# Two message-passing layers over 100,000 nodes: the destination rows gathered in the first pass, and its segment sums in another bank

## The reference, cut to what matters

```
h = relu(layernorm(x))                       # every node
f_s, f_v = linear maps of h                  # lin1
msg  = products of f[src], edge_attr, MLP(edge scalars)
mid  = segment_sum(msg, dst) / 4
conv = linear map of mid                     # lin2
angle = 0.1 * (mid_s @ lin3) / sqrt(96) * attr
x = x + cos(angle) * (linear map of h) * attr + sin(angle) * conv
h = relu(layernorm(x))
m = products of h[src], edge_attr, five weight matrices
x = x + h + relu(linear map of segment_sum(m, dst))
```

## Time and profile before

| | |
|---|---|
| time, median of 3 runs | 2462.75 us (2461.12 to 2464.57) |
| profiled execution | 2464.93 us, span 2463.1 us |
| busy: PE, DVE, ACT, POOL | 1773.9, 1866.4, 1350.1, 1483.3 us |
| mean granted clock of TensorE | 0.89 |

### The profile page before, as it was taken

The page is one execution under the profiler, slowest core; times in us unless marked ns, Lnnn a source line. Parts: engine busy times, 40 slices in busy tenths (PEclk is TensorE's granted clock), DMA queues, the critical chain, the costliest instruction groups (busy, mean ns, idle before and its releaser), DMA issues. The chain is left out here.

```text
span 2463.1 us, 51415 instructions
## 1 busy us (share of the span) xinstructions
PE 1773.9 (72%) x12130; PEld 1620.2 (66%) x12130; DVE 1866.4 (76%) x6716; ACT 1350.1 (55%) x3801; POOL 1483.3 (60%) x1436
## 2 busy tenths in 40 slices
PE   6788888888888888888886544545444777777776
PEld 2777777777777777777775544444444666666665
DVE  1799999999999999999996766666664555656554
ACT  2466666666666666666665645555553444444443
POOL 2345455454555545555454777777776777767775
PEclk9999999999999999999998555555555999999999
DMA  5355555555555555555554333333333333333332
GB/s 184 128 188 206 200 192 193 185 205 200 195 194 184 203 200 198 194 182 202 200 201 165 118 107 113 113 116 121 116 107 93 99 97 105 108 102 109 108 105 72
DMA packets 162656, 376.27 MB, mean 153 GB/s; under 512 B 42142, under 2 KB 72092, under 8 KB 162462
## 3 DMA queue, kind: packets, MB, share of 16 engines
q1 hardware_dynamic: 115582, 301.58, 34.7%
q0 software_dynamic: 47040, 74.31, 11.4%
HBM read 182.72 MB, written 200.80 MB: 156 GB/s over the span
## 5 line engine op out<-in xcount | busy, mean ns | idle before, releaser
L651 POOL TENSOR_TENSOR yo<-x,h 128x640 f32<-128x640 f32 x196 | 303.7, 1550 | 506.0 <-ACT h L774 504.8
L985 PE MATMUL bank<-wp,hT 128*128 128x160 f32 x1568 | 376.3, 322 | 0.0
L774 ACT ACTIVATE h<-x,nmr,inv 128x160 f32<-128x160 f32 x784 | 342.1, 514 | 1.5 <-DVE nmr L1211 1.5
L985 PE MATMUL bank<-wp,eT 128*128 128x160 f32 x784 | 263.6, 429 | 49.9 <-ACT eR L897 43.7
L610 POOL DMA_INDIRECT out<-yo,i_put x196 | 209.1, 1067 | 119.2 <-issue 80.7
L604 POOL DMA_INDIRECT x_e<-in_xa,i_src x196 | 217.3, 1109 | 98.7 <-issue 47.2
L1354 DVE SCALAR_TENSOR_TENSOR x<-bank,scl,x_all 128x160 f32<-128x160 f32 x784 | 256.3, 365 | 5.1 <-PE bank L986 2.6
L610 POOL DMA_INDIRECT h_all<-h,i_put x196 | 223.9, 1142 | 59.8 <-issue 58.6
L986 PE MATMUL bank<-wp,hR 128*128 128x64 f32 x1568 | 259.3, 247 | 0.0
L986 PEld LDWEIGHTS bank<-wp,hR 128*128 128x128 f32 x1568 | 255.5, 190 | 0.0
L980 PE MATMUL bank<-ident,h_e 128*128 128x128 f32 x392 | 83.6, 351 | 223.4 <-DVE hr_e L1526 223.0
(11 more groups left out here) (163 smaller groups left out, 5537.8 us busy)
## 6 DMA issues: line engine op xcount, KB each, us to landing
x_all<-in_xa SPq DMA_DIRECT2D x98, 644.0 KB, 5.0
h_all<-h SPq DMA_DIRECT2D x98, 640.0 KB, 3.0
out<-yo SPq DMA_DIRECT2D x98, 640.0 KB, 3.4
q_row<-row_tab SPq DMA_DIRECT2D x98, 256.0 KB, 3.6
sum_tab<-tot SPq DMA_DIRECT2D x49, 322.0 KB, 4.2
y_tab<-yo SPq DMA_DIRECT2D x49, 320.0 KB
x<-y_tab SPq DMA_DIRECT2D x49, 320.0 KB
cv<-sum_tab SPq DMA_DIRECT2D x25, 322.0 KB, 3.1
```

What stands on the lines that cost most here:

```text
L651: nc.gpsimd.tensor_tensor(yo[j][:, a:b], x1[j][:, a:b], h1[j][:, a:b], ALU.add).then_inc(d_y, 1)
L774: ins = nc.scalar.activation(h1[j][:, k * D:(k + 1) * D], x1[j][:, k * D:(k + 1) * D], ACT.Relu, bias=nmr2[j][:, k:k + 1], scale=inv2[j][: ...
L985: nc.tensor.matmul(dst_ps, main[:, t * P:(t + 1) * P], wp[:, w:w + D], start=True, stop=False)
```

## The change

Four edits. The segment sum of tile n goes to columns 0 to 160 of bank 5 or 6, by the tile's parity, the bank of the products of tile n+2, which are read out by then; the waits that bank 1 needed go, and two others come. The gathers of destination rows go from GpSimd's second pass to its odd step of the first pass, behind centre and scale, into a new tile `x_d` with two buffers; VectorE copies their indices at the end of an odd step, and SP stores a quad of them in a new table `own_tab`. In the second pass SP loads a quad of `own_tab` with one DMA, and GpSimd only scatters. `dense_y` does each half in two instructions of 320 columns in place of one of 640.

```diff
+    own_tab = scratch("own_tab", (Q, P, GQ * XW))
...
-        i_dst = four("i_dst", [P, GQ], i32)
+        i_dst = two("i_dst", [P, GQ], i32)
...
+        x_d = two("x_d", [P, GQ * XW])
@@ SP @@
+            def own_store(q):
+                j = q.mod(2)
+                sp.wait_ge(o_g[j], q.over(2, 64, 64))
+                sp.dma_start(own_tab[q.times(1)], x_d[j][:, :]).then_inc(o_st[j], 16)
...
                 if v.mod(2) == 1 and (q - 2).within(Q):
                     p1_store(q - 2)
+                    own_store(q - 2)
...
                 sp.wait_ge(e_st[j], 16 * ((Q + 1 - j) // 2))
+                sp.wait_ge(o_st[j], 16 * ((Q + 1 - j) // 2))
+            sp.wait_ge(d_x1, 4 * U)
+            def p2_own(q):
+                k = q.mod(4)
+                wait(sp, r_x1, q.times(2, -6))
+                sp.dma_start(x_q[k], own_tab[q.times(1)]).then_inc(r_g[k], 16)
...
             def p2_step(v):
+                if v.within(Q):
+                    p2_own(v)
@@ GpSimd @@
+            def own_gather(q):
+                j = q.mod(2)
+                pool.wait_ge(o_ix, q.times(1, 1))
+                wait(pool, o_st[j], q.over(2, 16))
+                gather(xa, x_d[j], XW, i_dst[j], o_g[j])
...
             def dense_y(u):
...
-                    a, b = h * GQ * D, (h + 1) * GQ * D
-                    nc.gpsimd.tensor_tensor(yo[j][:, a:b], x1[j][:, a:b], h1[j][:, a:b], ALU.add).then_inc(d_y, 1)
+                    for k in (2 * h, 2 * h + 1):
+                        a, b = 2 * k * D, 2 * (k + 1) * D
+                        ins = nc.gpsimd.tensor_tensor(yo[j][:, a:b], x1[j][:, a:b], h1[j][:, a:b], ALU.add)
+                    ins.then_inc(d_y, 1)
...
                 if w.mod(2) == 1 and (q + 1).within(Q):
                     p1_centre(q + 1)
                     p1_scale(q + 1)
+                if w.mod(2) == 1 and (q - 1).within(Q):
+                    own_gather(q - 1)
...
-                    p2_gather(w)
@@ ACT, p1_total @@
-                nc.scalar.activation(tot[j][:, t * CW:(t + 1) * CW], bank[1][:, U_SEG:U_SEG + CW],
+                nc.scalar.activation(tot[j][:, t * CW:(t + 1) * CW], bank[5 + n.mod(2)][:, 0:CW],
@@ TensorE, dense_tr, p1_tr, p1_source, p1_sum @@
-                wait(pe, e_tot, u.times(2, h - 2))
...
-                wait(pe, e_tot, q.times(4, -4))
...
+                wait(pe, e_tot, n.times(1, -3))
...
-                wait(pe, d_hT, dense_copied)
+                pe.wait_ge(e_ft, n.times(1, 3) if (n + 2).within(T) else T)
+                total = bank[5 + n.mod(2)][:, 0:CW]
@@ VectorE, step @@
+                if u.mod(2) == 1 and (q1 - 1).within(Q):
+                    wait(v, o_g[(q1 - 1).mod(2)], (q1 - 1).over(2, 64))
+                    index_copy(i_dst[(q1 - 1).mod(2)], t_gat, q1 - 1, o_ix)
@@ VectorE, p2_stats @@
-                v.wait_ge(r_g[q.mod(4)], q.over(4, 64, 64))
+                v.wait_ge(r_g[q.mod(4)], q.over(4, 16, 16))
@@ VectorE, p2_step @@
-                if (q + 3).within(Q):
-                    index_copy(i_dst[(q + 3).mod(4)], t_gat, q + 3, r_ix)
```

More of the change, by code:

```diff
@@ L38 @@
 U_C, U_A, U_D, U_B = 0, 32, 97, 193
-U_SEG = 2 * P
 class At:
@@ L305, in gnn_kernel @@
         e_st = sem2("p1_sum_stored")
-        r_ix = sem("p2_index_copied")
+        o_ix = sem("own_index_copied")
+        o_g = sem2("own_rows_gathered")
+        o_st = sem2("own_rows_stored")
         r_px = sem("p2_put_copied")
         r_cv = [sem(f"p2_sums_loaded{i}") for i in range(4)]
-        r_g = [sem(f"p2_node_rows{i}") for i in range(4)]
+        r_g = [sem(f"p2_own_rows_loaded{i}") for i in range(4)]
         r_ln1 = sem("p2_moments1")
@@ L692, in _ @@
                 step(At(0, w))
[L695 to L699, removed]
             def p2_scatter(q):
@@ L706, in p2_scatter @@
                     scatter_tile(h1_all, h1[j][:, t * D:(t + 1) * D], i_put[q.mod(4)], t, r_put[j])
-            def p2_step(w):
-                if w.within(Q):
-                    p2_gather(w)
[L712 to L717, removed]
             for j in range(2):
@@ L720, in _ @@
                 pool.wait_ge(d_sto[j], 16 * (U // 2))
-            with pool.Fori(1, Q // 4) as i:
+            with pool.Fori(0, Q // 4) as i:
                 for c in range(4):
-                    p2_step(At(i, c))
-            for w in range(Q - 1, Q + 4):
-                p2_step(At(0, w))
+                    p2_scatter(At(i, c))
+            p2_scatter(At(0, Q - 1))
             for j in range(2):
@@ L1064, in p1_source, with p1_sum @@
                                  start=True, stop=True).then_inc(e_pw, 1)
-            def p1_sum(n, dense_copied):
+            def p1_sum(n):
                 j, t = n.c // GQ % 2, n.mod(4)
@@ L1072, in p1_sum @@
                 wait(pe, e_tot, n.times(1))
-                wait(pe, d_hT, dense_copied)
+                pe.wait_ge(e_ft, n.times(1, 3) if (n + 2).within(T) else T)
+                total = bank[5 + n.mod(2)][:, 0:CW]
                 before = tot[j][:, (t - 1) * CW:t * CW] if t else tot[1 - j][:, (GQ - 1) * CW:GQ * CW]
-                nc.tensor.matmul(bank[1][:, U_SEG:U_SEG + CW], same[j][:, t * P:(t + 1) * P], v_e[n.mod(2)][:, :],
+                nc.tensor.matmul(total, same[j][:, t * P:(t + 1) * P], v_e[n.mod(2)][:, :],
                                  start=True, stop=False)
-                nc.tensor.matmul(bank[1][:, U_SEG:U_SEG + CW], carry[j][:, t * P:(t + 1) * P], before,
+                nc.tensor.matmul(total, carry[j][:, t * P:(t + 1) * P], before,
                                  start=False, stop=True).then_inc(e_seg, 1)
@@ L1103, in slot @@
                 if (s - 3).within(T):
-                    p1_sum(s - 3, u.times(2, h) if u.within(U) else 2 * U)
+                    p1_sum(s - 3)
             def step(u):
@@ L1663, in p2_step @@
                     p2_angle(q, 7)
-            for q in range(3):
-                index_copy(i_dst[q], t_gat, At(0, q), r_ix)
             v.wait_ge(d_y, 2 * U)
```

## The result

Over ten runs each, 2463.89 us before and 2470.43 us after: a ratio of 1.0033, with a 95% interval of 1.0023 to 1.0042. The change made the kernel 0.3% slower; 2433 us was forecast. Its profiled execution has a span of 2467.1 us, against 2463.1.

The account below looks back on a forecast made before the run. GpSimd's in-order queue was taken to close the first pass's loop and pace the second pass. First pass +108, between passes +6, second pass -144 give -30 us: 2433 us forecast, range 2365 to 2520.

Parts of the forecast that it names:

- The loop: First pass: E, ACT's even h1, y, centre, scale, gathers, odd y, E; 25.61 us a turn before, 28.0 forecast.
- the waits: First pass: VectorE waits for y 3 to 6 us a turn; TensorE's four 0.58 us waits on sums go.
- the second pass: GpSimd's queue sets its pace; without gathers, steps of 7.6 us, 386.9 us in all, -144 us.
- E: First pass: the moment VectorE begins an even unit step, which follows GpSimd's y of the odd unit.
- Rival A: First pass: the added gathers hide and freed TensorE waits count, 1.6 us a turn; 2253 us; chance 0.10.
- C: Second pass stays as long because something other than GpSimd's queue sets its pace; 2577 us; chance 0.06.
- E to y is 9.8 us: First pass: from E to GpSimd's even-unit y, 3.76 + 5.86 us plus 0.15 for handovers; 12.98 before.
- rival B: First pass: VectorE's wait at E idles TensorE, whose clock halves; up to 3 us a turn, 2568 us; chance 0.24.
- The 6 us between the passes: Between last y and second pass: the last own rows must be stored and loaded; +6 us, between 2 and 10.
- 29.1 us with 6.45 for both gathers: First-pass turn if selector and centring hold GpSimd's issues, by the Trainium skill's SBUF rule, instead of 28.0.
- the turn's upper bound: First-pass turn from above: 29.6 us, with 6.45 for both gathers and E to y of 10.5.
- the scales at 1361.77: Second pass: called the fourth step's scales, 19.7 us after its start, followed by 45 steps of 7.6 us.

Follow-up runs that it names:

- whole y: The changed kernel with each y in one instruction as before, that part undone; its four runs took 2396, 2399, 2463 and 2470 us.

## Why the prediction was wrong

*The loop, the order, the waits, the second pass: right.* E stands 16.45 us behind the centring by the forecast's own terms (3.1 + 6.45 + 5.35 + 1.75 + 0.1 - 0.3), and 16.45 on average in the trace. That the two are equal to the digit is luck: the own gathers took 6.39 us where 5.35 stood, the source gathers 5.24 where 6.45 stood. VectorE waits for y (7.3 us a turn, more than the 3 to 6 named), the waits on the sums are gone, the second pass is 2.5 us off in 144. Rival A fell (VectorE waits in each turn), and so did C.

*The step that failed is "E to y is 9.8 us".* It measures 10.9 on average. With 1.1 us more the turn is 29.0 and not 28.0, the pass 46 us longer than forecast, and the 30 us that were to be gained are gone. The 9.8 was worked out from rows at full clock, and without the clock's fall it is less: 9.1 to 9.3 us in 20 turns with twelve matmuls, 9.1 in the turn shown with whole y. So rival B's mechanism is in the change, in every turn, at some 1.7 us; its full price was 3, and its sign, a granted clock below 1, is there (0.90). By estimate, with 9.2 the turn would have been 29.0 - 1.7 = 27.3 us, and the kernel about 48 x 1.7 = 82 us faster than it is, 2388 us; the profiled kernel with whole y, at 2396, has that stretch and a turn of 27.2, though its clock falls elsewhere. I gave B 0.24 because TensorE would still be busy for 21 of 28 us. That was the wrong quantity: it was busy 80% of the time, and the clock fell in 39 of 39 turns with its idle time in one piece of 4.3 us, in 6 of 39 with it in several. The Trainium skill ("TensorE: Matmul & The Clock Gate", "HAM oscillation — how this bites in real kernels") describes a loop whose wait re-throttles TensorE in each iteration; this trace agrees: idle from 727 to 730.5, then 1.2 GHz, in every turn.

*The bank part, in the other direction.* The prediction takes 0.58 us out of the stretch for it. Removing waits from an engine that must wait at E anyway moves them there: four times 0.58 and a 1.1, 3.4 us in all, became one stall of 4.3 us in a turn 0.9 us longer, and the clock fell. Alone the part gains 84 us, inside the change it costs 30.

*Small terms.* The 6 us between the passes did not come: -0.5. The third pass is 7.7 us shorter though nothing in it changed; its clock was at half for some 16 of its first 20 us, and for its first 30 before the change. The range, 2365 to 2520, held the time. The other turn that the working gives, 29.1 us with 6.45 for both gathers, comes close to 29.0 by luck: the two took 11.6 us together and not 12.9. Slips of the working move nothing: the terms of the turn's upper bound make 29.8 and not 29.6, the chances outside the range 0.28 and not two in ten, and the scales at 1361.77 are those of the third step, with 45 steps from there to the last but one.

What stays open: why the kernel with whole y takes 2396 us in one run and 2470 in another, why the clock fell behind one stall of 2.3 to 2.6 us and not behind another, and what lengthens the turns at full clock with the gathers moved and the sums in bank 1.

## What to carry to other kernels

Where work is put into one engine's queue inside a loop, find the engines that will wait for it and see whether TensorE's idle time comes in one piece: a TensorE that is 80% busy ran at half clock for a fifth of the time (a mean of 0.90). A removed wait is worth what the loop's own end allows; priced inside a change it can have the other sign than alone. The same four issues cost 232 us between scale and y and 35 us split over the two gaps where GpSimd waited for h1 anyway, so look for the gap before the price.

## What the runs showed of the hardware that was not expected

Twelve matmuls that nobody reads made a kernel 28 us faster, and six 43 us, by the clock. And a meeting of GpSimd and VectorE on SBUF, 1.65 us long, cost 3.0 to 4.2 us a turn: 1.3 to 1.5 of itself, and the rest by way of a TensorE stall and its clock.
